# Two draining passes in another order, and the last sequence's end in two halves of 256 tokens

## The reference

```python
# block 1: x + attn(layernorm(x))
xk, xv, xr = (x * m + shift(x) * (1 - m) for m in (mix_k, mix_v, mix_r))
k, v, r = xk @ Wk.T, xv @ Wv.T, xr @ Wr.T
y = wkv(w, time_first, k, v)             # running maximum, two decayed sums, a quotient per token
x = x + (sigmoid(r) * y) @ Wo.T
# block 2: x + ffn(layernorm(x))
xc = silu(pointwise(conv3_causal(x)))    # depthwise convolution of 3 taps, then 256x256
x1 = x + xc
rw = top2_softmax(x1 @ router_w.T + router_b)          # 8 experts, 2 used per token
ye = silu(x1 @ expert_w[e].T + expert_b[e])            # all 8 are computed
h = rmsnorm(x1 + sum_e(rw[e] * ye[e]) @ out_w.T + out_b)
out = h + gelu(h @ ff_down.T + b) @ ff_up.T + b
```

## Time and profile before

| | us |
|---|---|
| median of three runs (lowest, highest) | 968.68 (964.82, 970.49) |
| profiled execution | 964.94 |
| its span, first to last instruction | 963.1 |
| PE busy in the span | 879.4 |
| DVE busy | 854.9 |
| ACT busy | 719.3 |
| mean granted clock of PE, as a share of full speed | 0.976 |

### The profile page before, as it was taken

The page is one execution under the profiler, slowest core; times in us unless marked ns, Lnnn a source line. Parts: engine busy times, 40 slices in busy tenths (PEclk is TensorE's granted clock), DMA queues, the critical chain, the costliest instruction groups (busy, mean ns, idle before and its releaser), DMA issues. The chain is left out here.

```text
span 963.1 us, 15789 instructions
## 1 busy us (share of the span) xinstructions
PE 879.4 (91%) x4288; PEld 481.6 (50%) x4288; DVE 854.9 (89%) x1579; ACT 719.3 (75%) x1233; POOL 220.8 (23%) x472
## 2 busy tenths in 40 slices
PE   2567999999999999999999999999999999969895
PEld 1233555555545555555545555554555555535542
DVE  6997999999999999999999999999999999947562
ACT  4748687887878787886878788787878788545642
POOL 4260413131141403222141313114140320111000
PEclk9788999999999999999999999999999999989997
DMA  6110100102010100101010010101010000100000
GB/s 214 45 44 1 45 1 14 54 1 66 0 65 0 49 16 0 65 0 65 0 65 0 10 55 0 65 0 65 0 48 18 23 23 1 45 1 22 1 22 22
DMA packets 28772, 29.66 MB, mean 31 GB/s; under 512 B 2090, under 2 KB 28484, under 8 KB 28484
## 3 DMA queue, kind: packets, MB, share of 16 engines
q1 hardware_dynamic: 28740, 29.27, 9.1%
HBM read 20.87 MB, written 8.39 MB: 30 GB/s over the span
## 5 line engine op out<-in xcount | busy, mean ns | idle before, releaser
L1288 DVE SCALAR_TENSOR_TENSOR comb<-ye,rw,comb 128x256 f32<-128x256 f32 x448 | 216.3, 483 | 24.5 <-ACT ye L715 10.5
L715 ACT ACTIVATE ye<-pe 128x512 f32<-128x512 f32 x256 | 151.1, 596 | 110.1 <-PE pe L454 98.2
L454 PE MATMUL pe<-weh,x1l 128*128 128x512 f16 x512 | 194.0, 379 | 0.0
L453 PE MATMUL pe<-wel,x1h 128*128 128x512 f16 x512 | 194.0, 379 | 0.0
L452 PE MATMUL pe<-weh,x1h 128*128 128x512 f16 x512 | 194.0, 379 | 0.0
L450 PE MATMUL pe<-brow,ones 128*128 128x512 f16 x256 | 97.1, 379 | 18.1 <-ACT ye L715 18.1
L405 POOL TENSOR_TENSOR msv<-ms,rms_eps_c 128x2 f32<-128x2 f32 x32 | 10.2, 320 | 406.3 <-ACT sq L735 406.3
L376 POOL TENSOR_TENSOR mo<-st 128x4 f32<-128x4 f32 x32 | 20.5, 642 | 305.4 <-DVE st L1092 196.8
L454 PEld LDWEIGHTS pe<-weh,x1l 128*128 128x128 f16 x512 | 50.1, 98 | 60.4
L453 PEld LDWEIGHTS pe<-wel,x1h 128*128 128x128 f16 x512 | 50.0, 98 | 60.5
L452 PEld LDWEIGHTS pe<-weh,x1h 128*128 128x128 f16 x512 | 50.1, 98 | 50.5
(11 more groups left out here) (152 smaller groups left out, 1947.9 us busy)
## 6 DMA issues: line engine op xcount, KB each, us to landing
xa<-in_x SPq DMA_DIRECT2D x16, 512.0 KB, 3.5
xres<-in_x SPq DMA_DIRECT2D x16, 512.0 KB, 4.6
out_y<-yo SPq DMA_DIRECT2D x16, 512.0 KB, 2.9
ye<-in_w_expert SPq DMA_DIRECT2D x2, 1024.0 KB, 7.9
wa<-in_w_attn SPq DMA_DIRECT2D x1, 1024.0 KB, 11.6
wpw<-in_w_pw SPq DMA_DIRECT2D x1, 256.0 KB, 10.9
wout<-in_w_out SPq DMA_DIRECT2D x1, 256.0 KB, 6.5
wdown<-in_w_down SPq DMA_DIRECT2D x2, 64.0 KB, 5.1
```

The source lines that it names most:

```text
L453: nc.tensor.matmul(dst, x1h[:, h, tok], wel[:, h, cols], start=False, stop=False)
L454: mm = nc.tensor.matmul(dst, x1l[:, h, tok], weh[:, h, cols], start=False, stop=h == H - 1)
L715: act.activation(ye[:, i % NY, :], pe[:, i % 2, :], ACT.Silu, scale=1.0 / WSCALE).then_inc(ye_ready.sem, 1)
L1288: v.scalar_tensor_tensor(out=comb[:, t, :], in0=src, scalar=rw[:, t, e:e + 1], in1=comb[:, t, :], op0=ALU.mult, op1=ALU.add).then_inc(comb ...
```

## The change

Three things are changed, all of them after the hardware loop.

1. The convolution of sequence b moves in the passes 12 and 13 from behind expert tile 14 to behind tile 13.
2. In pass 13 `reciprocal()`, with its table load, moves to the head of ACT's pass; a second load brings the silu table back.
3. For the last sequence (15) the end runs in two halves of 256 tokens. Already in pass 14 the squares of the first half go ahead of the last silu, DVE scales the first half ahead of the last expert tile's sums, and the third `comb` tile is transposed and copied. In pass 15 transposes, `ht` copies, down matmul, gelu, copies, remainder, up matmul, last sum and store are each done twice on 256 tokens, in a written order; the gelu table is loaded at the head of the pass; the transposes go to the accumulator `pk` and the down product to `pe` instead of `pt`.

The diff:

```diff
+        def is_last(seq):
+            return isinstance(seq, int) and seq == B - 1
+        HT = T // 2
+        front, back = slice(0, HT), slice(HT, T)
         def is_first(seq):
...
                     sp.dma_start(xres[:], dram_seq(x_tok, a)).then_inc(xres_in.sem, 16)
-                if on(g):
+                if is_last(g):
+                    for i in range(2):
+                        sp.wait_ge(y_ready.sem, y_ready.at(g, i + 1))
+                        t = slice(2 * i, 2 * i + 2)
+                        sp.dma_start(dram_seq(out_tok, g)[:, t, :], yo[:, t, :]).then_inc(stored.sem, 16)
+                elif on(g):
                     sp.wait_ge(y_ready.sem, y_ready.at(g))
...
             schedule(sp, body, {-3: gather_biases})
-            sp.wait_ge(stored.sem, stored.at(B - 1))
+            sp.wait_ge(stored.sem, stored.at(B - 1, 2 * 16))
...
+                def turn_half(i):
+                    te.wait_ge(h_ready.sem, h_ready.at(g, 2 * i + 2))
+                    te.wait_ge(s1_ready.sem, s1_ready.at(g))
+                    te.wait_ge(logits_read.sem, logits_read.at(g))
+                    for h in range(H):
+                        for t in range(2 * i, 2 * i + 2):
+                            mm = nc.tensor.transpose(pk[:, h, t * P:(t + 1) * P], hh[:, t, h * P:(h + 1) * P], ident[:])
+                    mm.then_inc(t4_done.sem, 1)
+                def down_half(i, cols):
+                    te.wait_ge(ht_ready.sem, ht_ready.at(g, i + 1))
+                    te.wait_ge(ye_ready.sem, ye_ready.at(g, NT * NG - 1))
+                    for h in range(H):
+                        mm = nc.tensor.matmul(pe[:, 0, cols], wdown[:, h, :], ht[:, h, cols], start=h == 0,
+                                              stop=h == H - 1)
+                    mm.then_inc(down_done.sem, 1)
+                def up_half(i):
+                    te.wait_ge(ffh_ready.sem, ffh_ready.at(g, 2 * i + 2))
+                    te.wait_ge(ffl_ready.sem, ffl_ready.at(g, i + 1))
+                    for t in range(2 * i, 2 * i + 2):
+                        dst = po[:, i, t % 2, :]
+                        nc.tensor.matmul(dst, ffs[:, t * P:(t + 1) * P], wuh[:], start=True, stop=False)
+                        mm = nc.tensor.matmul(dst, ffh[:, t * P:(t + 1) * P], wul[:], start=False, stop=True)
+                    mm.then_inc(up_done.sem, 1)
+                if is_last(g):
+                    turn_half(0)
+                    turn_combined(g, 3)
+                    mix_out(g, 1)
+                    down_half(0, front)
+                    turn_half(1)
+                    up_half(0)
+                    down_half(1, back)
+                    up_half(1)
+                    return
                 if on(a):
...
                     mix_out(f, 0)
+                    if is_last(f):
+                        turn_combined(f, 2)
                     experts(3, (3,))
...
                     copy_k()
+                if is_last(g):
+                    act.preload_act_table_set("gelu_and_others")
+                    for i, cols in ((0, front), (1, back)):
+                        act.wait_ge(t4_done.sem, t4_done.at(g, i + 1))
+                        act.wait_ge(down_done.sem, down_done.at(g - 1))
+                        act.copy(ht[:, :, cols], pk[:, :, cols]).then_inc(ht_ready.sem, 1)
+                        if i == 0:
+                            copy_combined(g, 3)
+                            squares(g, 1)
+                            act.wait_ge(ffl_ready.sem, ffl_ready.at(g - 1))
+                            act.wait_ge(up_done.sem, up_done.at(g - 1))
+                        act.wait_ge(down_done.sem, down_done.at(g, i + 1))
+                        act.activation(ffg[:, cols], pe[:, 0, cols], ACT.Gelu, bias=bdown[:, 0:1]).then_inc(ffg_ready.sem, 1)
+                        act.wait_ge(ffg_ready.sem, ffg_ready.at(g, i + 1))
+                        act.copy(ffs[:, cols], ffg[:, cols]).then_inc(ffh_ready.sem, 1)
+                        act.copy(ffh[0:HID, cols], ffg[0:HID, cols]).then_inc(ffh_ready.sem, 1)
+                    return
+                if draining and on(b):
+                    act.preload_act_table_set("natural_log_exp_and_others")
+                    reciprocal()
+                    act.preload_act_table_set("silu_and_others")
                 if on(g):
...
                     pointwise_silu(1)
-                    if on(b):
-                        act.preload_act_table_set("natural_log_exp_and_others")
-                        reciprocal()
                 if on(a):
...
                         fade(2, 1)
-                    silus(3, (3,))
-                    squares(f, 0)
+                    if is_last(f):
+                        squares(f, 0)
+                        copy_combined(f, 2)
+                        silus(3, (3,))
+                    else:
+                        silus(3, (3,))
+                        squares(f, 0)
...
-                def last_sum():
-                    dve.wait_ge(xh_ready.sem, xh_ready.at(g))
+                def last_sum(halves=range(2)):
+                    dve.wait_ge(xh_ready.sem, xh_ready.at(g, halves[-1] + 1 if is_last(g) else 1))
                     if on(g - 1):
...
                         dve.wait_ge(stored.sem, stored.at(g - 1))
-                    for i in range(2):
+                    for i in halves:
                         dve.wait_ge(up_done.sem, up_done.at(g, i + 1))
...
-                def scale_h(i):
+                def scale_h(i, seq=g):
-                    dve.wait_ge(rms_ready.sem, rms_ready.at(g, 3 * i + 3))
+                    dve.wait_ge(rms_ready.sem, rms_ready.at(seq, 3 * i + 3))
-                    if on(g - 1):
-                        dve.wait_ge(t4_done.sem, t4_done.at(g - 1))
-                        dve.wait_ge(xh_ready.sem, xh_ready.at(g - 1))
+                    if on(seq - 1):
+                        dve.wait_ge(t4_done.sem, t4_done.at(seq - 1))
+                        dve.wait_ge(xh_ready.sem, xh_ready.at(seq - 1))
                     for t in range(2 * i, 2 * i + 2):
...
+                def add_half(seq, i):
+                    dve.wait_ge(h_ready.sem, h_ready.at(seq, 2 * i + 2))
+                    dve.wait_ge(x2t_ready.sem, x2t_ready.at(seq))
+                    if on(seq - 1):
+                        dve.wait_ge(y_ready.sem, y_ready.at(seq - 1))
+                    t = slice(2 * i, 2 * i + 2)
+                    v.tensor_tensor(xh[:, t, :], x2t[:, t, :], hh[:, t, :], ALU.add).then_inc(xh_ready.sem, 1)
+                def low_half(i, cols):
+                    dve.wait_ge(ffh_ready.sem, ffh_ready.at(g, 2 * i + 1))
+                    v.tensor_tensor(ffs[HID:, cols], ffg[HID:, cols], ffs[HID:, cols], ALU.subtract).then_inc(ffl_ready.sem, 1)
+                if is_last(g):
+                    scale_h(1)
+                    low_half(0, front)
+                    add_half(g, 1)
+                    last_sum((0,))
+                    low_half(1, back)
+                    last_sum((1,))
+                    return
                 if on(a):
...
                                 stats_proj()
-                            if on(b) and not on(n) and i == 14:
+                            if on(b) and not on(n) and i == 13:
                                 convolve(b)
+                            if is_last(f) and i == 14:
+                                scale_h(0, f)
                             if on(g) and i == 4:
...
                                 mix(n, 1, xv)
-                else:
-                    last_sum()
+                    if is_last(f):
+                        add_half(f, 0)
```

## The result

The changed kernel takes 958.41 us in the median of six runs (956.14 to 962.95), the kernel before 967.3 us in six (963.75 to 970.49): a ratio of 0.9909 with a 95% interval of 0.9886 to 0.9931. A second set on another occasion gave 958.4 us and 0.991 (0.9885 to 0.9936). The profiled run fell from 964.94 to 956.83 us and its span from 963.1 to 955.0, by 8.1 us.

The account below looks back on a forecast made before the run. In draining passes PE stands still between expert tiles, waiting on DVE and ACT; the last 23 us are one chain. Pass 13's -3.4 and the end's -4.4 gave -7.8 us; forecast 960.5 us, own range 957.0 to 963.8, overall 956.0 to 966.0.

Parts of the forecast that it names:

- The convolution: Head of pass 13: convolution starts 1.04 us sooner, PE's idle shrinks from 3.12 to 2.1 us; 0 at pass 13's end.
- The reciprocal: Head of pass 13 on ACT: `mix_out` 0.6 us earlier, `ht` at 857.8 instead of 860.36, -2.5 us.
- The clock in pass 13: PE in pass 13: -4.2 us if the clock stays up, -0.8 if it falls, weighed to -3.4 us.
- The rival: Clock falls in pass 13's new 2.3 us gap before `mix_out`: pass 13 gives -0.8, run 964.3 us; chance 0.12.
- The halves: Last sequence's end in two halves: -5.2 us at full rate, -3.6 at the lower rate, taken as -4.4 us.
- The bound of -3.6: Last sequence's end with PE at the lower rate: ends at 959.5 against 963.1 us, a gain of 3.6 us.
- Two loads that each hold ACT for twice their row: ACT's head of pass 13 ends 2 x 1.28 us later, pass 13 gains nothing: 964.3 us; chance 0.05.
- the halves don't pay: Last sequence's end: fixed costs make each half step take the whole's time, end at 963.5, nothing won; chance 0.10.
- the slower one: PE at half rate through pass 13's head and the end: +3.7 us, 972.4 us; chance 0.05.
- The sum: Pass 13's -3.4 plus the end's -4.4 gives -7.8 us, profiled run from 964.94 to 957.1 us.

Follow-up runs that it names:

- convolution alone: Kernel before with only the convolution moved one tile sooner: median 962.65 us, ratio 0.9963.
- reciprocal alone: Kernel before with only the reciprocal moved to the head of ACT's pass 13, one load added: median 962.45 us, ratio 0.9966.
- both edits: Kernel before with convolution and reciprocal moved and the end undivided: median 963.31 us, ratio 0.9963 to before.
- gap filled: Kernel after plus nine idle matmuls in PE's wait for combt in pass 13: median 959.08 us, ratio 0.9924 to the kernel before.
- the halves alone: Kernel after with convolution and reciprocal put back, only the end in halves new: median 961.02 us, ratio 0.9949 to the kernel before.

## Why the prediction was right, point by point

- **The convolution.** Its step was right as far as it went: PE's wait 2.01 us (2.1 forecast), no effect at the end of pass 13 (S14 the same). That "the reciprocal eats nearly half" of it was too kind: it eats more than all of it. `mix_out` starts 6.85 us behind the silu wherever the reciprocal stands at the head of the pass, against 5.86 with nothing moved and the first pointwise product at full rate, and 4.72 with the convolution alone. It comes 0.46 us sooner than before (0.6 forecast) only because in the profiled run of before that product ran at the low clock (3.25 us).
- **The reciprocal.** ACT was free at 849.83, 6.33 us behind the silu, against 850.7 - 844.49 = 6.2 forecast; `ht` follows the transposes, the down matmul took 1.98 us, `x1l` was not late. All this came out.
- **The clock in pass 13.** This is the term that was off: -3.4 forecast, -2.4 in the profile. The rival priced a fall in the new gap at -0.8 for the pass, which took it that the down matmul would then stay slow as well. Its own price of 1.7 us off the -4.2 would have been -2.5, and that is what came: -4.0 without a fall (reciprocal alone, both edits, gap filled; forecast -4.2), -2.4 with one, since the down matmul recovers either way. What it did not price is that the 23.95 it started from held a lost clock of its own, in the first pointwise product: 1.5 us that the same instructions did not lose in another profile (22.43). A wait of 2.40 us kept the clock in one run and one of 2.41 us lost it in two, and behind the old wait of 3.12 to 3.14 us it fell in two and stayed in two, so no length of wait alone decides.
- **The halves.** -4.4 forecast between -3.6 and -5.2, -4.7 measured, and -3.0 to -3.6 in three other profiles where the clock fell somewhere in the last pass. Step by step from 939.93 or 936.57: second `hh` ends +0.99 us (forecast 0.98); second down matmul starts 0.50 us later (0.46); from gelu to the up matmuls 1.51 us (1.4). The whole last pass ran at full rate, for which the sum had -5.2; the 0.5 us missing are small terms set too short, the down product to the gelu (1.17 us against 1.0), the up matmuls to the last sum (0.74 against 0.6) and the gelu's 0.1. The bound of -3.6 was too near, since the fall can also hit the last `mix_out` (2.02 us in two runs), which the sum had at full rate. DVE's timeline of after, which answers to the earlier trace rows:

```profile
946.12 0.88 DVE L1185 SCALAR_TENSOR_TENSOR hh<-po,rms,normw 128x256 f32<-128x256 f32 x2 [4.77 <-POOL rms L420]
...
951.80 0.69 DVE L1158 SCALAR_TENSOR_TENSOR yo<-po,xh 128x512 f32<-128x512 f32 x1 [0.89 <-PE po L596]
```

  And ACT's, the second half's gelu, which answers to the earlier trace rows:

```profile
949.55 0.47 ACT L903 ACTIVATE ffg<-pe,bdown 128x256 f32<-128x256 f32 x1 [1.22 <-PE pe L585]
950.05 0.40 ACT L905 CAST ffs<-ffg 128x256 f16<-128x256 f32 x1
```

  The last sum ends at 952.49, and 2.51 us later the program (2.5 forecast).
- **Two loads that each hold ACT for twice their row.** Excluded: both loads of pass 13 end 0.01 us ahead of the next instruction (844.99 + 1.28 to 846.28, 848.54 + 1.28 to 849.83), and the instruction ahead of each ends 0.02 to 0.03 us before it starts (844.77 + 0.19 to 844.99, 847.46 + 1.06 to 848.54). That leaves no room for the drain that the Trainium skill ("ScalarE: Activation LUTs", section "What ACT_TABLE_LOAD costs") adds to a switch.
- **The other rivals.** That the halves don't pay is excluded by the halves alone (S15 19.59). For the slower one the clock would have had to stay low over most of pass 13's chain; it was at 0.50 from 850.5 to 853.5 and back at full for the product behind.
- **The sum.** -7.8 forecast, -7.1 in the stretches the change touches, -8.9 between the medians (-6.7 to -11.0 by the interval). The -7.1 lies within that interval; that the rest is the scatter of S0 and of the clock is not shown, as the kernel before has one profile. That the sum came so near is in part luck: both terms stood between a figure at the full and one at the low clock, and the profile has one of each, pass 13 with a fall and the end without.

## What to carry to other kernels

An instruction group moved to the head of an engine's pass becomes the wait of everything queued behind it: here `mix_out` came 6.85 us behind the silu with the reciprocal at the head and 4.76 with it in the next wait. Check what the next engine wants first, and move into the wait behind that instead. Two edits that each take away one wait on the same chain don't add up when the second puts a new wait at the first one's place. Where engines run one after another, price each stretch at both levels of PE's clock: in the last 23 us here the clock was worth as much as the overlap. And take more than one profile of the kernel before: one stretch of it varied by 1.5 us with nothing changed.

## What the runs showed of the hardware

All seven waits that were filled with idle matmuls (in three profiles) were followed by work at the full rate. The plainest case is the old end: behind 3.30 us of idle PE the down product took 3.78 us in four profiles of four, and in the one profile with twelve idle matmuls of 2.75 us in that wait it took 1.98 us. Elsewhere the same wait ended both ways without any filling: behind 3.12 to 3.14 us the first pointwise product took 3.25 and 3.15 us in two profiles and 1.98 in two others, and behind 0.73 us pass 14's down matmul took 3.48 to 3.68 us in three profiles and 1.98 or 1.99 in the others. So the instructions ahead of it do not fix whether the clock falls; what decides is not shown here. Half-width steps cost more than half: gelu 0.47 against 0.69 us, the two stores of 256 KB 2.1 us from issue to landing against 2.9 for one of 512 KB.
